# Where half a tile's sums are added: an image-and-text attention kernel with another fold, another place for a pair of matmul groups, and another ring

## The reference

```python
ctx_img = context[:, :IMG_TOKENS]
ctx_txt = context[:, IMG_TOKENS:]
q = rms_norm(x @ w_q.T + b_q, g_q)
k, v = rms_norm(ctx_txt @ w_k.T + b_k, g_k), ctx_txt @ w_v.T + b_v
k_img, v_img = rms_norm(ctx_img @ w_k_img.T + b_k_img, g_k_img), ctx_img @ w_v_img.T + b_v_img
img_x = attention(q, k_img, v_img)
txt_x = attention(q, k, v, kv_mask)
out = (txt_x + img_x).reshape(b, -1, DIM)
return out @ w_o.T + b_o
```

## Time and profile before

| | us |
|---|---|
| median of three runs | 3315.51 |
| lowest, highest | 3306.97, 3318.33 |
| profiled execution | 3314.12 |
| its span, first to last instruction | 3312.3 |
| mean granted clock of PE | 0.957 |

### The profile page before, as it was taken

One profiled execution on the slowest core, in us unless ns is written; L12 is line 12 of the kernel. 1 busy time (PEld: TensorE's weight loads), 2 busy tenths in 40 slices (PEclk: granted clock), 3 DMA queues, 4 the chain that ended last, 5 costly groups with the idle time before them and its releaser, 6 DMA issues. The chain is left out here.

```text
span 3312.3 us, 52045 instructions
## 1 busy us (share of the span) xinstructions
PE 3008.0 (91%) x15500; PEld 1888.7 (57%) x15500; DVE 2107.4 (64%) x4449; ACT 1621.5 (49%) x3005; POOL 1404.1 (42%) x577
## 2 busy tenths in 40 slices
PE   7999999999699999999999999999993588999991
PEld 6777777877444444444444444444431466777771
DVE  5666666666577777767767777777743774443435
ACT  3343334333166666666666666666663653222222
POOL 0000000000067877877877877877873261000000
PEclk9999999999699999999999999999996699999996
DMA  6677777767946676676676776776635261000005
GB/s 171 150 165 165 162 161 165 169 146 156 185 90 123 129 147 127 125 147 116 136 141 114 145 139 116 145 143 112 144 55 146 80 201 32 0 1 0 0 0 203
DMA packets 377445, 401.97 MB, mean 121 GB/s; under 512 B 48304, under 2 KB 298224, under 8 KB 369016
## 3 DMA queue, kind: packets, MB, share of 16 engines
q1 hardware_dynamic: 363272, 323.61, 41.2%
q0 software_dynamic: 9728, 67.12, 14.9%
q10 hardware_dynamic: 4224, 8.39, 0.7%
HBM read 210.77 MB, written 121.15 MB: 100 GB/s over the span
## 5 line engine op out<-in xcount | busy, mean ns | idle before, releaser
L1011 ACT ACTIVATE at_probs<-at_st 128x512 f32<-128x512 f32 (+1 forms) x1664 | 931.4, 597 | 554.2 <-PE at_st L849 533.9
L1041 DVE TENSOR_REDUCE at_cm<-at_mx 128x1 f32<-128x448 f32 x1536 | 855.8, 617 | 339.8 <-PE at_mx L869 336.6
L802 POOL TENSOR_TENSOR at_added<-at_added,at_probs 128x2048 f32<-128x2048 f32 x192 | 889.2, 4631 | 11.5
L849 PE MATMUL at_st<-at_qst,at_kst 101*128 101x512 f32 (+1 forms) x1664 | 651.2, 431 | 9.2 <-ACT at_probs L1011 5.8
L869 PE MATMUL at_mx<-at_kst,at_qst 97*128 97x448 f32 (+1 forms) x2048 | 621.0, 378 | 33.1 <-DMA at_kst<-stack_rows 24.1
L849 PEld LDWEIGHTS at_st<-at_qst,at_kst 101*128 101x128 f32 (+1 forms) x1664 | 295.2, 186 | 438.9 <-ACT at_probs L1011 308.1
L869 PEld LDWEIGHTS at_mx<-at_kst,at_qst 97*128 97x128 f32 x2048 | 398.7, 195 | 192.8 <-DVE at_cm L1041 117.6
L893 PE MATMUL at_acc<-at_probs,at_vt 128*32 128x512 f32 (+2 forms) x3584 | 477.8, 607 | 3.0 <-ACT at_probs L1011 3.0
L770 POOL MEMSET at_ones<- 128x32 f32 x1 | 0.1, 129 | 826.5 <-POOLq L302 826.5
L802 POOL TENSOR_TENSOR at_added<-at_probs 128x2048 f32<-128x2048 f32 x32 | 146.3, 4571 | 307.3 <-PE at_mx L908 251.6
L1555 ACT ACTIVATE ff_h<-ff_psa,ff_b1c,alpha 128x512 f32<-128x512 f32 x128 | 99.5, 778 | 344.6 <-PE ff_psa L1532 344.6
(11 more groups left out here) (205 smaller groups left out, 4710.5 us busy)
## 6 DMA issues: line engine op xcount, KB each, us to landing
at_kst<-k_high SPq DMA_DIRECT2D x256, 200.0 KB
at_probs<-at_probs POOLq DMA_DIRECT2D x32, 1024.0 KB, 7.0
at_kst<-k_low SPq DMA_DIRECT2D x128, 200.0 KB
pj_xin<-in_ctx_dram SPq DMA_DIRECT2D x96, 256.0 KB, 4.4
k_high<-pj_kh SPq DMA_DIRECT2D x96, 256.0 KB, 3.3
k_low<-pj_kl SPq DMA_DIRECT2D x96, 256.0 KB, 4.9
values<-pj_vs SPq DMA_DIRECT2D x96, 256.0 KB, 4.8
at_vt<-values SPq DMA_DIRECT2D x32, 768.0 KB
```

What stands on the lines that cost most here:

```text
L802: pool.tensor_tensor(added[:], so_far, probs[:, SLOT[t]], ALU.add).then_inc(S["add_done"], 1)
L849: pe.matmul(st[0:kn, bank, :], kst[g.j][:, h, t * P:t * P + kn], qst[g.j][:, h, :], start=True, stop=True).then_inc(S["st_done"], 1)
L1011: act.activation(probs[0:kn, SLOT[t], h, :], st[0:kn, (NST * g.j + HG * t + h) % 3, :], ACT.Exp, scale=SCALE).then_inc(S["exp_done"], 1)
L1041: dve.tensor_reduce(dst, mx[:, bank % 4, 0:kn], AX.X, ALU.max, negate=last).then_inc(S["mx_free"], 1)
```

## The change

The text half of tile 10 is added into tile 6 and no longer into `added`, behind the landing of the fold of tile 5 (the wait for `folded[0]`). POOL issues it before the addition of tile 9 (`FOLD_BEFORE`). The image sums come at the end of tile 3. Tile 3 takes slot 0 of the ring and tile 4 slot 3, where it was the other way round. `join` goes behind the third addition, and the copy of the image sums behind tile 4, head 0. In the last group POOL issues no folds: PE sums all tiles itself, four for the text and three for the image.

```diff
-    FOLDS = [(5, 0, P, 6), (10, 0, HALF, None), (10, HALF, P, 11)]
+    FOLDS = [(5, 0, P, 6), (10, 0, HALF, 6), (10, HALF, P, 11)]
     SUMMED = [[(6, 0, P), (None, 0, P)], [(12, 0, KLAST), (11, 0, P)]]
-    SUMS_AFTER = {1: 0, 2: 1}
+    SUMMED_LAST = [[(5, 0, P), (6, 0, P), (10, 0, HALF), (None, 0, P)], [(10, HALF, P), (12, 0, KLAST), (11, 0, P)]]
+    FOLD_BEFORE = {7: 0, 9: 1}
+    SUMS_AFTER = {1: 0, 3: 1}
...
-    JOIN_AT = 2
+    JOIN_AT = 3
...
-    SLOT = [0, 1, 2, 3, 0, 1, 2, 4, 5, 0, 3, 4, 5]
+    SLOT = [0, 1, 2, 0, 3, 1, 2, 4, 5, 0, 3, 4, 5]
...
             def fold(g, n):
                 t, r0, r1, into = FOLDS[n]
                 pool.wait_ge(S["exp_done"], NST * g.G + HG * (t + 1))
-                if into is None:
-                    pool.wait_ge(S["add_done"], NADD * (g.G + 1))
-                    dst = added[r0:r1]
-                else:
-                    pool.wait_ge(S["v_done"], NPASS * g.G + max(q for q in range(NPASS) if PASS[q][0] == into) + 1)
-                    dst = probs[r0:r1, SLOT[into]]
+                pool.wait_ge(S["v_done"], NPASS * g.G + max(q for q in range(NPASS) if PASS[q][0] == into) + 1)
+                if n == 1:
+                    pool.wait_ge(folded[0], 16 * (g.G + 1))
...
-                    if TEXT[n + 1] == 7:
-                        fold(g, 0)
+                    if not g.last and TEXT[n + 1] in FOLD_BEFORE:
+                        fold(g, FOLD_BEFORE[TEXT[n + 1]])
                     add(g, n)
-                fold(g, 1)
                 if not g.first:
                     scale(g.at(-1))
-                fold(g, 2)
+                if not g.last:
+                    fold(g, 2)
...
                 if q == 0:
-                    pe.wait_ge(folded[0], 16 * (g.G + 1))
-                    pe.wait_ge(folded[1], 16 * (g.G + 1))
                     pe.wait_ge(S["add_done"], NADD * (g.G + 1))
-                else:
-                    pe.wait_ge(folded[2], 16 * (g.G + 1))
-                for k, (t, r0, r1) in enumerate(SUMMED[q]):
+                if not g.last:
+                    pe.wait_ge(folded[q + 1], 16 * (g.G + 1))
+                tiles = SUMMED_LAST[q] if g.last else SUMMED[q]
+                for k, (t, r0, r1) in enumerate(tiles):
...
-                            if (t, h) == (3, 1):
+                            if (t, h) == (4, 0):
                                 evacuate(before, SI)
```

More of the change, by code:

```diff
@@ L821, in fold @@
                 pool.sem_inc(S["fold_ready"], 1)
-                pool.dma_start(dst, probs[r0:r1, SLOT[t]], accum_op=ALU.add).then_inc(folded[n], 16)
+                pool.dma_start(probs[r0:r1, SLOT[into]], probs[r0:r1, SLOT[t]], accum_op=ALU.add).then_inc(folded[n], 16)
             def body(g):
@@ L907, in sums @@
                         src = added[:, h, :] if t is None else probs[r0:r1, SLOT[t], h, :]
-                        done = pe.matmul(mx[cols, bank, :], ones[r0:r1, :], src, start=k == 0, stop=k == 1)
+                        done = pe.matmul(mx[cols, bank, :], ones[r0:r1, :], src, start=k == 0, stop=k == len(tiles) - 1)
                 done.then_inc(S["s_done"], 1)
```

## The result

| | before | after |
|---|---|---|
| median, us | 3314.57 (9 runs) | 3297.79 (9 runs) |
| lowest, highest | 3306.97, 3318.33 | 3292.17, 3303.24 |
| span of the profiled execution | 3312.3 | 3299.1 |

The ratio of the times is 0.9957, with a 95% interval of 0.9948 to 0.9966: 0.43% off, which is 14 us. The medians alone lie 17 us apart. Of the 29 us that the forecast promised, about half came. The forecast of 3286 us was 12 us too low; the direction held, and the time lies inside the range near its upper end.

A forecast was written before the change was run, and what follows sets the result against it. PE was taken to set the pace, losing time to a fold DMA issued too late. Waits -17.7, group 0 +1, end -11, clock -1 sum to -28.7 us: forecast 3286 us, range 3271 to 3301.

The forecast's parts named there:

- The waits in front of the sums: PE's idle time before both sums, 0.57 us a group over 31 groups, goes: -17.7 us, bounds 11 to 32.
- DVE's share: 5.2 of the 16.6 us PE idles before the sums, read as the same wait as the late DMA landing.
- the signs given for "wrong": PE waiting for ACT at tile 3's fourth score, for DVE over 0.3 us at image sums, or stage clock under 0.98.
- "I take nothing" for tile 3: ACT's new 0.8 us stall on tile 3's first exponential stays hidden by 0.8 us of room: cost zero.
- "PE sets the pace; the other three engines have room": Attention stage, 960 to 2456 us: PE busy 1459.31 of 1496 us, POOL 1222.40, DVE 1080.76, ACT 978.43.
- The rival of the stall: Tile 3's ACT stall reaches PE, in full 25 us, in full or half 3298 to 3311 us; chance 0.10.
- Group 0: With no sums to cover it, its third tile waits for the group's first addition: +1 us once.
- The last group: Sums start earlier, no folds, seven passes on PE: -11 us, range 8 to 14.
- 13 was the bound: Sign of being right: in the last group the sums end within 13 us of the last addition.
- The clock: Falls to half clock inside the stage stay, but for 1 us: -1 us.
- the slow rival: ACT's late start at tile 3 makes the clock fall often, about 3 us each; 20 falls give 3346 us; chance 0.04.
- the rival by which the falls go with the waits: Idle time before the sums lets the clock fall, so 7 us more go: 3279 us; chance 0.10.

The follow-up runs named there:

- the fold alone: Kernel before, with only the text half of tile 10 folded into tile 6 ahead of the addition of tile 9: 3284.78 us, ratio 0.9914.
- The first kernel with short reductions: Changed kernel, with each DVE reduction of a text chunk's maxima reading only 224 of its 448 columns: 3196.35 us, ratio 0.9649.
- the old ring: Changed kernel with tile 3 back in slot 3 and tile 4 in slot 0, nothing else: 3292.30 us, ratio 0.9939.
- the old places: Changed kernel with the maxima where they were (tiles 1 and 2 at places 0 to 3), new slots kept: 3275.16 us, ratio 0.9890.
- the kernel with the last group alone: Kernel before, with only the last group changed: no folds in it, seven passes of sums on PE: 3305.11 us, ratio 0.9976.
- the nine kernels with full reductions: The follow-up kernels, parts of the change or variants of it, that compute every maximum in full: 3274.19 to 3306.53 us.

## Why the prediction was right or wrong

**The waits in front of the sums: right in place and kind.** Their cause was a DMA issued too late; both parts that move it away, each alone, bring the image sums to 0.29 us behind the matmul before them in all groups from 3 to 30. Reading DVE's share of the earlier trace rows as the same wait was right too: it went with the fold. The price was near, even low: the fold alone shortened the mean group by 0.69 us, 21 us for 31 groups, where 17.7 stand in the sum and 11 to 32 in its bounds. None of the signs given for "wrong" appeared: PE does not stand idle before the image sums, and the granted clock of the stage is 0.99. The part that failed had no sign of its own.

**"I take nothing" for tile 3: this failed, and by another mechanism than the rival's.** The sum has every part that waits, and none for what else `SUMS_AFTER` steers. I saw the swapped layouts, wrote "Tile 3 now has the layout that tile 2 has before", and took from it that the fourth score would come 2.83 us after the first. It came 2017.79 - 2014.64 = 3.15 us after. A layout has no duration of its own; it depends on how full DVE's queue is when it begins. Before, the text sums, 1.85 us of PE without maxima, stood directly ahead of the tile with maxima at places 0 to 3. Here are DVE's rows around that tile, before:

```profile
2017.70 0.78 DVE L1041 TENSOR_REDUCE at_top<-at_mx 128x1 f32<-128x257 f32 x2
2020.55 1.69 DVE L1041 TENSOR_REDUCE at_cm<-at_mx 128x1 f32<-128x448 f32 x3 [2.06 <-PE at_mx L869]
2022.83 1.16 DVE L1041 TENSOR_REDUCE at_cm<-at_mx 128x1 f32<-128x448 f32 x2 [0.60 <-PE at_mx L869]
```

And after:

```profile
2009.16 0.78 DVE L1039 TENSOR_REDUCE at_top<-at_mx 128x1 f32<-128x257 f32 x2
2013.65 3.28 DVE L1039 TENSOR_REDUCE at_cm<-at_mx 128x1 f32<-128x448 f32 x6 [3.72 <-PE at_mx L868]
2016.85 0.75 DVE L1039 TENSOR_REDUCE at_top<-at_mx 128x1 f32<-128x257 f32 x2
2017.99 1.16 DVE L1039 TENSOR_REDUCE at_cm<-at_mx 128x1 f32<-128x448 f32 x2 [0.39 <-PE at_mx L868]
```

Before, DVE comes to the tile after 2.06 us of idleness, and has three reductions and a pause. After, it stands idle for 3.72 us, through the text sums and the first half of tile 2, where no maxima come; then it has eight reductions without a pause, since tile 2's maxima now lie at that tile's end and tile 3's follow directly. The matmuls of one maximum stand 0.2 to 0.3 us apart, DVE needs 0.6 us for each, and there are four banks: once they are full, PE goes at DVE's pace. Tiles 2 to 4 together take 3.39 + 5.53 + 3.31 = 12.23 us after, against 5.20 + 3.39 + 3.21 = 11.80 with the fold alone: 0.43 us a group, **13 us in groups 1 to 30**. That it nearly equals the 12 us by which the forecast was too low is partly luck, as the sum at the end of this section shows.

**"PE sets the pace; the other three engines have room": the sentence at the root of it.** By the stage's sums DVE had 28% of room. The first kernel with short reductions shows what that is worth: 615 ns down to 384 ns gives 101 us, 3.1% of the program. DVE's busy share says nothing about the moments at which PE wants a bank. The waits were there before, 99.0 us of them, as a row of the view that I had read for POOL and ACT alone:

```profile
PEld at_mx L869 <- DVE at_cm L1041: 99.0, 339, 0.3
```

The Trainium skill, "VectorE: DVE Perf Modes", section "Rules for kernel authors", calls the reduction the slowest operation of DVE and advises to restructure where it lies on the hot path. The 101 us agree with the advice. That it is the slowest operation this trace does not show: DVE's reciprocal of 512 columns takes 3352 ns here. The rows add the cost: 448 columns take 615 ns and 224 columns 384, so 224 columns cost 231 ns and each reduction some 150 ns besides.

**The rival of the stall: wrong.** ACT does wait for POOL, 26 times and 36 us in all, about as often as said. The 1.38 us of group 22 hold 0.54 us in which ACT waits for the score with the old ring too, so the stall itself is 0.84 us, and 0.8 had been said. Tile 3 takes as long without the new ring, in the changed layout (5.53 us) and in the old one (5.17), where DVE does not hold PE up at that place. That the banks and the sums behind it let ACT catch up, as the step said, fits; it was not tested by itself.

**Group 0: +1.3 us for +1, and not settled.** It takes 51.4 us with the old ring and 50.8 with the old places, which would point to both. But in the kernel with the last group alone, where group 0 is that of before, it takes 51.9. One profile each does not tell 1 us.

**The last group: -7.5 us for -11.** The seven passes behave as said. The last four additions and the sums behind them, in the changed kernel:

```profile
2479.73 18.62 POOL L804 TENSOR_TENSOR at_added<-at_added,at_probs 128x2048 f32<-128x2048 f32 x4
...
2499.47 4.93 PE L906 MATMUL at_mx<-at_probs,at_ones 128*32 128x512 f32 x24
2504.33 1.07 PE L906 MATMUL at_mx<-at_added,at_ones 128*32 128x512 f32 x8
2505.32 2.92 PE L906 MATMUL at_mx<-at_probs,at_ones 64*32 64x512 f32 x24
```

The last addition ends at 2498.35, the last sum at 2508.24: 10 us, where 13 was the bound. What failed is the start: the text sums began at 2457.95, 9.1 us after the group's first exponential and not 5.7, and POOL's first addition 11.9 us after it instead of 7.9. The granted clock was 0.50, the 1.2 GHz level, through the tiles ahead of it, and again under most of the first three of the seven passes (columns as in the earlier trace rows):

```profile
2445.70:2459.40 13.70, 13.42 (x50) 3.57 (x46) 0.00 (x0) 6.05 (x12) 5.01 (x3) 0.50 0.74 87
2490.00:2503.70 13.70, 12.49 (x49) 2.35 (x52) 0.00 (x0) 4.32 (x9) 9.44 (x3) 0.50 0.05 19
```

I took the 3.23 us of the wait off the old start, 2464.91, and put no term for a low clock ahead of the sums. In the kernel with the old places, where the last group has no low clock until 2464.1, it takes 64.0 us; with the old ring and the rest of the change, where it begins only 33 us into the group, the group takes 65.9 us, 11.6 less than before. So the term that was mis-sized here is, as far as these three show, the clock ahead of the sums, which the forecast had at nothing.

**The clock: the falls at the start of a round stayed, as taken; one behind a wait went.** In groups 1 to 30 there are 17.1 us at low clock before and 16.8 after, in groups 1 to 29 17.0 and 13.6. Nor did the falls become frequent, as the slow rival had it. But one of the three falls before, at 1574.1 us, comes right behind a wait in front of the image sums, and it is of a kind that no kernel without these waits has. First those sums, then the fall:

```profile
1573.61 3.23 PE L908 MATMUL at_mx<-at_probs,at_ones 65*32 65x512 f32 x16 [1.40 <-DMA at_probs<-at_probs]
```

```profile
1574.10:1577.50 3.40, 3.40 (x18) 0.92 (x10) 0.00 (x0) 0.00 (x0) 3.40 (x1) 0.50 1.02 264
```

The kernel with the last group alone, which has the waits too, shows the same at 2028.3 us, 0.9 us behind sums that had waited 1.16 us. So, as far as two instances show, the rival by which the falls go with the waits was right for this kind, which cost 1.3 us (3.23 us for sums that take 1.93), and wrong for the others. The two kernels with the waits have 3 and 4 falls up to group 29, the nine without them 1 to 3; one profile each does not show whether the waits bring others too. The Trainium skill, "TensorE: Matmul & The Clock Gate", section "Why this matters for your kernels", names idle gaps between bursts of matmuls as what sends the clock back, but longer ones than any that PE has here from group 3 to 29 (1.40 us at most before, 0.40 after). The falls here come behind shorter ones; their rows stand above and in the last section.

**Together,** by the kernels that did one part: in groups 1 to 30 the waits -21 and the maxima +13, the last group -7.5, group 0 +1.3, the program behind the stage +1.5, which is -12.7 us; the two profiled executions lie 13.2 us apart. The medians lie 17 us apart, since the profiled execution of after, 3300.92 us, was 3.1 us above its median. (The forecast's own sum gives 3286.8 us, not 3286.) The step that made the forecast miss is the term of zero for the maxima, 13 us; the 3.5 us that the last group brought less and the 1.5 behind the stage add to it, and the waits, worth 3 us more than forecast, hid a part.

## What to carry to other kernels

Before a step is moved, look up every use of the table that moves it: here the sums' table also placed work for another engine, and that cost more than half of what the move was to bring. An engine at 72% over a stage can still set the pace where its work comes in bursts that are longer than the buffers between it and its producer; read PE's weight-load waits by name, and lay the consumer's pauses (its idle before each run of work) beside the producer's. And of two cures for one wait take the one that moves least: the earlier fold alone beat the whole change, and with the maxima left in place the change gives 1.1%, where it gave 0.4.

## What the runs showed of the hardware

Most falls of the clock within the stage are bound to a place. The changed kernel's first one, by windows, and PE just ahead of it:

```profile
1507.00:1513.80 6.80, 6.80 (x24) 3.89 (x28) 3.73 (x8) 2.86 (x6) 0.00 (x0) 0.50 0.99 139
```

```profile
1505.26 0.73 PE L848 MATMUL at_st<-at_qst,at_kst 101*128 101x512 f32 x2 [0.38 <-issue]
1505.92 2.91 PE L892 MATMUL at_acc<-at_probs,at_vt 64*32 64x512 f32 x16
```

PE is busy through the whole fall and stood idle for 0.38 us ahead of it, 1.7 us before it began. The fall begins 1.0 us behind the first exponential of group 12, and its second one 1.1 us behind that of group 27. Over before, after and the nine kernels with full reductions there are 20 falls before group 30: 18 of them begin 0.7 to 2.1 us behind the start of a group whose number is a multiple of three, where a round of the hardware loop begins, with a gap of 0.3 to 0.4 us in PE's work 1.5 to 2.8 us ahead of them. The other two are of 3.4 us and are the ones behind the waits in front of the image sums, at 1574.1 us before and at 2028.3 us with the last group alone; each also follows 65 us on another fall. Most rounds have none. A group with a fall of 6.8 us is 2.7 to 2.9 us longer than those at the same place of a round without one, and 2.0 to 2.1 us in the two kernels with the waits. Why one round has it and the next has not, no run shows.

The landing of a half-tile DMA depends on what was issued ahead of it: 512 KB landed 12.4 us after the issue when another 512 KB had been issued 1.8 us before, and after 8.0 us, the median over both, once the last addition stood between them (7.6 us with the fold alone).
